# Layer 3 of a four-layer model on one core: convolutions on TensorE, two features spread by one-hot products, another order of the two lanes

## The reference, cut to what matters

```python
def _L3_attn_ref(x, ...):
    u = _rmsnorm(x, norm1_w)
    uc = conv(u, dw_kernel, 4 taps, causal, one filter per feature) + dw_bias
    xh = (uc @ pw_w.T + pw_b).reshape(b, l, 16, 8)
    xp = einsum('blhd,kd->blhk', xh, x_proj_w)          # dt_x (8), Bx (48), Cx (48)
    dt = softplus(einsum('blhr,dr->blhd', dt_x, dt_proj_w) + dt_proj_b)
    A = -exp(A_log)
    for t in range(l):
        h = exp(dt[t] * A) * h + (dt[t] * xh[t]) * Bx[t]
        y[t] = sum_s(h * Cx[t])
    x1 = x + (y @ out_proj_w.T + out_proj_b)
    h2 = _rmsnorm(x1, norm2_w)
    return x1 + (silu(h2 @ gate_w.T) * (h2 @ up_w.T)) @ down_w.T
```

## Time and profile before

| | |
|---|---|
| median of 3 runs | 2117.89 us (2117.66 to 2123.4) |
| the profiled execution | 2106.99 us |
| its span, first to last instruction | 2105.2 us |
| TensorE's mean granted clock | 0.883 of full speed |
| DMA | 113.66 MB, mean 54 GB/s |
| instructions | 28567 |

### The profile page before, as it was taken

How to read it: one execution, slowest core, us unless ns; L and a number is a source line. 1 busy time by engine, 2 the same in 40 slices (tenths; PEclk the granted TensorE clock), 3 DMA queues, 4 the chain that set the end, 5 groups by cost and what they waited for, 6 DMA issues and landing times.

```text
span 2105.2 us, 28567 instructions
## 1 busy us (share of the span) xinstructions
PE 1642.7 (78%) x10505; PEld 944.0 (45%) x10546; DVE 1371.6 (65%) x3084; ACT 909.8 (43%) x1592; POOL 799.0 (38%) x670
## 2 busy tenths in 40 slices
PE   6797698667878778876768788779768887688667
PEld 3455565112555566423335566524315455564114
DVE  4664355999554455787985435488896544467996
ACT  3462233554435333544535352344544542335553
POOL 2411101995222121373652221165571421025892
PEclk9999898777989899888889998979879998899788
DMA  6005301410000341202100312220210023302210
GB/s 197 1 1 158 99 2 35 135 41 9 13 0 1 99 129 31 85 21 64 52 1 11 99 31 61 74 93 9 85 31 6 1 59 93 98 10 85 75 52 11
DMA packets 96589, 113.66 MB, mean 54 GB/s; under 512 B 7616, under 2 KB 70848, under 8 KB 96192
## 3 DMA queue, kind: packets, MB, share of 16 engines
q1 hardware_dynamic: 94400, 107.63, 17.1%
q0 software_dynamic: 2048, 4.20, 0.7%
HBM read 88.86 MB, written 22.94 MB: 53 GB/s over the span
## 4 chain that ended last, share of the span: by engine, by line
PE 46%; DVE 19%; POOL 9%; ACT 8%; issue 7%; DMA 6%; SPq 6%; DVEq 0%; ACTq 0%; POOLq 0%
PE P L228 9%; POOL M L2079 6%; DVE M L2009 6%; PE P L1634 4%; PE P L1842 3%; SPq L1457 3%; PE P L1217 2%; SPq L1458 2%; DMA W<-in_e 2%; PE P L962 2%; PE P L2137 1%; PE P L390 1%; DMA M<-du 1%; PE P L1222 1%; PE P L217 1%
## 5 line engine op out<-in xcount | busy, mean ns | idle before, releaser
L2009 DVE TENSOR_TENSOR_SCAN M<-P,M 128x512 f32<-128x512 f32 x384 | 446.5, 1204 | 30.2 <-POOL M L2079 18.8
L1842 PE MATMUL P<-M,wt 32*32 32x512 f32 x3072 | 272.4, 780 | 144.7 <-DVE M L2009 108.4
L1923 ACT ACTIVATE P<-M,negA 128x512 f32<-128x512 f32 x384 | 264.2, 690 | 228.9 <-DVE M L2009 213.9
L228 PEld LDWEIGHTS P<-wt,M 128*128 128x128 f32 x2176 | 275.7, 193 | 97.1 <-issue 34.6
L228 PE MATMUL P<-wt,M 128*128 128x128 f32 x2176 | 289.8, 279 | 15.0 <-ACT M L1930 3.4
L2079 POOL TENSOR_TENSOR M<-M 128x512 f32<-128x512 f32 x192 | 244.0, 1305 | 138.0 <-DMA M<-du 76.1
L2079 POOL TENSOR_TENSOR M<-W,M 128x512 f32<-128x512 f32 x192 | 242.3, 1297 | 56.7 <-PE P L1842 56.5
L1842 PEld LDWEIGHTS P<-M,wt 32*32 32x32 f32 x3072 | 40.1, 117 | 330.3 <-DVE M L2009 259.0
L209 POOL TENSOR_TENSOR st<-st,wt 128x4 f32<-128x4 f32 x64 | 84.7, 1323 | 255.9 <-DVE st L192 255.5
L1731 DVE TENSOR_TENSOR M<-M,P 128x512 f32<-128x512 f32 x128 | 87.4, 683 | 93.0 <-PE P L1642 64.5
L1634 PE MATMUL P<-M,wt 128*128 128x512 f32 x256 | 138.0, 623 | 11.0 <-ACT M L1683 6.2
(11 more groups left out here) (338 smaller groups left out, 3236.0 us busy)
## 6 DMA issues: line engine op xcount, KB each, us to landing
W<-in_e SPq DMA_DIRECT2D x152, 192.0 KB
M<-dt SPq DMA_DIRECT2D x64, 256.0 KB, 5.2
M<-xs SPq DMA_DIRECT2D x32, 256.0 KB, 4.2
ys<-M SPq DMA_DIRECT2D x32, 256.0 KB, 2.3
M<-du SPq DMA_DIRECT2D x32, 256.0 KB, 4.9
W<-du SPq DMA_DIRECT2D x32, 256.0 KB, 6.0
W<-xh SPq DMA_DIRECT2D x16, 256.0 KB
xs<-zero SPq DMA_DIRECT2D x2, 1216.0 KB, 10.7
```

Source lines behind the costliest of these rows:

```text
L228: m = e.matmul(out[:, tok(j)], h[:, tok(j)], wgt, start=first and j == 0, stop=last, skip_group_check=True)
L1842: m = e.matmul(t["sums"][i // 2][to:to + 32, :], part("WC", c)[r, r], scan[r, :], start=c == 0, stop=c == 5, tile_position=(32 * i, to))
L1923: e.activation(t["aa"][n % 2][:, :], t["dtr"][i][:, :], EXP, scale=negA[:, c:c + 1]).then_inc(ACT.s, ACT.mark(b, "a3", "aa", n))
L2009: e.tensor_tensor_scan(bb[:, :], t["aa"][n % 2][:, :], bb[:, :], 0.0, MUL, ADD).then_inc(DVE.s, DVE.mark(b, "a3", "scan", n))
```

## The change

- The weights of the two convolutions are multiplied once, on DVE, into four matrices `cw` (one for each tap), and the two biases into one column `cb`. PE then computes xh with four products of `cw` and `up`, shifted by 0 to 3 columns, summed in PSUM. L1959 and L1964 go.
- ABS reads PSUM with the bias itself; z is computed behind the exponential and no longer stands ahead of it. The load of the table is issued behind xh. The last DVE steps of softplus are in another order.
- All six chunks of B are copied by ACT.
- The first two features (k = 0) of dt and du are spread by PE: products of one-hot matrices `spread` (256 columns of weights more) with `dt` and `du`, in P[0] and P[2], copied by ACT (`dtr`) and DVE (`dub`). `sp_attn3` reads back only features 2 and 3 at first.
- The bits in `TURNS` are new for all engines. "Lane 0 is favoured" means that its steps stand ahead more often.

```diff
+        cw, cb = sb("cw", [128, 512]), sb("cb", [128, 1])
@@ dve_consts
+                e.tensor_tensor(cb[:, :], L.P[3][:, 128:129], wv("pwb"), ADD).then_inc(DVE.s, DVE.mark("c", "conv"))
+                for k in range(4):
+                    e.tensor_scalar(cw[:, tok(k)], wv("pwT"), wv("dw")[:, k:k + 1], None, MUL).then_inc(
+                        DVE.s, DVE.mark("c", "conv"))
@@ pe_attn3
-            w.wait_ge(DVE.s, DVE.of(b, "a3", "conv", 3))
-            e.matmul(P[0][:, :], wv("pwT"), T_[10][:, :], start=True, stop=True).then_inc(PE.s, PE.mark(b, "a3", "xh"))
+            w.wait_ge(ACT.s, ACT.of(b, "a3", "yn"))
+            w.wait_ge(POOL.s, POOL.of(b, "a3", "pad"))
...
+            for k in range(4):
+                m = e.matmul(P[0][:, :], cw[:, tok(k)], up[:, k:k + T], start=k == 0, stop=k == 3)
+            m.then_inc(PE.s, PE.mark(b, "a3", "xh"))
...
+            for i in range(2):
+                yield
+                w.wait_ge(DVE.s, DVE.of(b, "a3", "dt"))
+                w.wait_ge(ACT.s, ACT.of(b, "a3", "dtr", 0) if i else ACT.of(b, "a3", "B", 2))
+                e.matmul(P[0][:, :], part("spread", i), T_[2][:, :], start=True, stop=True).then_inc(
+                    PE.s, PE.mark(b, "a3", "dtr", i))
+                yield
+                w.wait_ge(DVE.s, DVE.of(b, "a3", "du"))
...
+                e.matmul(P[2][:, :], part("spread", i), T_[3][:, :], start=True, stop=True).then_inc(
+                    PE.s, PE.mark(b, "a3", "dub", i))
@@ act_attn3
+            e.preload_act_table_set("natural_log_exp_and_others")
...
-            e.activation(T_[11][:, :], P[2][:, :], IDN, bias=wv("dtb")).then_inc(ACT.s, ACT.mark(b, "a3", "z"))
-            yield
-            w.wait_ge(ACT.s, ACT.of(b, "a3", "z"))
-            e.activation(T_[12][:, :], T_[11][:, :], ABS).then_inc(ACT.s, ACT.mark(b, "a3", "abs"))
+            e.activation(T_[12][:, :], P[2][:, :], ABS, bias=wv("dtb")).then_inc(ACT.s, ACT.mark(b, "a3", "abs"))
...
+            e.activation(T_[11][:, :], P[2][:, :], IDN, bias=wv("dtb")).then_inc(ACT.s, ACT.mark(b, "a3", "z"))
...
-            e.preload_act_table_set("natural_log_exp_and_others")
...
+            for i in range(2):
+                yield
+                w.wait_ge(PE.s, PE.of(b, "a3", "dtr", i))
+                e.activation(t["dtr"][i][:, :], P[0][:, :], COPY).then_inc(ACT.s, ACT.mark(b, "a3", "dtr", i))
@@ dve_attn3
+            for i in range(2):
+                yield
+                w.wait_ge(PE.s, PE.of(b, "a3", "dub", i))
+                e.tensor_copy(t["dub"][i][:, :], P[2][:, :]).then_inc(DVE.s, DVE.mark(b, "a3", "dub", i))
@@ sp_attn3
-            for q in range(4):
+            for q in range(2, 4):
                 spread(t["dtr"][q], dt_d[s], q, rep_dt[s][q])
                 spread(t["dub"][q], du_d[s], q, rep_du[s][q])
@@ TURNS, one row of "vector"
-                "9a5f5d740ff0017fffffffffff578c0be87bf480ffff9330b78000030a1fa80ee7ffdbdf3ed2405000028910f5ff3ffebffc"
+                "52dff73d55771682dfff578c0be87bf480fff87c85bf80000001e7f407e7fff5fe6ff030091204003bbf53ffebff39e0140a"
```

More of the change, by code:

```diff
@@ L1832, in gather @@
                 if g == 0:
-                    for i in (2, 3):
-                        w.wait_ge(ACT.s, ACT.of(b, "a3", "B", i))
+                    w.wait_ge(ACT.s, ACT.of(b, "a3", "dtr", 1))
+                    w.wait_ge(DVE.s, DVE.of(b, "a3", "dub", 1))
                 if k and c == 0:
@@ L1913, in decay @@
                 yield
[L1914 to L1918 removed]
+                if k == 0:
+                    w.wait_ge(ACT.s, ACT.of(b, "a3", "dtr", q))
+                elif q == i:
+                    w.wait_ge(rep_dt[b % 2][i], 16 * (b // 2 + 1))
+                else:
+                    w.wait_ge(rep_dt[b % 2][i], 16 * (2 * (b // 2) + k // 2 + 1))
+                if n == 0 and b < 2:
+                    w.wait_ge(DVE.s, DVE.of("c", "A"))
                 if n < 2:
@@ L2442, in layout @@
     add("sumd", sd)
+    add("spread", np.concatenate([(p[:, None] == p[None] // 8 * 8 + d).astype(f) for d in range(2)], 1))
     add("WB", np.concatenate([bd(xw[8 + 8 * c:16 + 8 * c].T) for c in range(6)], 1))
```

109 lines of the change are left out of this document (47 added, 62 removed).

## The result

The changed kernel takes 2067.64 us (median of 4 runs, 2064.99 to 2074.17), beside 2119.85 us for the kernel before on the same chip (4 runs, 2117.66 to 2123.4). The ratio is 0.9757, 95% interval [0.9738, 0.9776]: 52 us less. Forecast were 24 us less, 2096 us, with a range from 2062 to 2130. The sign is right, the size is under half of what came, and what the text called "a larger gain" (2070 us) is what was measured.

What follows compares the result with a forecast made beforehand. No engine is full throughout: the kernel changes between PE and DVE limits, with lanes waiting on their own chains between. Terms sum to -13.4 us, -21.4 with the order, giving 2096 us on the runs' scale; eight-in-ten range 2062 to 2130.

Steps and rivals of the forecast that it cites:

- a larger gain: Rival: the added products fall in PE's idle time, so the +26.8 us term is nothing; -48 us, 2070 us; chance 0.19.
- The ways: Layer 3 preparation, normalised input to first scan, six chain blocks: round trip -32.4, softplus -11.8, convolution +5.8 us.
- the convolution: Layer 3 preparation: four PE products replace DVE operations and one product, +1.0 us a block on the chain, +5.8 us.
- The round trip: Way from du to first scan: PE spreading replaces HBM, 9.4 to 4.0 us a block, -32.4 us; over 7 refutes.
- The softplus part: Layer 3 preparation: z and the table load leave the chain, 1.97 us in each of six blocks, -11.8 us.
- PE's share: PE's 56 added products, 58 us at 1.04 each, charged at PE's 0.46 of the chain: +26.8 us (0 to 43).
- The order: New instruction order: net 16 us less pause in one lane or the other, counted half: -8 us (-30 to +20).
- The pauses that the prediction counted: DVE order: block 3's sum no longer 40.5 us late; new pauses of 44 us at block 2's ffn3, 14.6 at block 0.
- DVE (-4.3) and ACT (+1.5): Work moved: DVE loses 22.5 us, charged at 0.19, -4.3 us; ACT gets 19 us at 0.08, +1.5 us.
- PE as the bound: Rival: 56 products cost in full beside the other lane's ffn2 and gathers; +20 to +56 us, 2148 us; chance 0.13.
- The trip was worth little: Rival: half the round trip's 32.4 us returns as another wait in the fixed order; -5 us, 2112 us; chance 0.14.
- That the new order loses: Rival: new pauses, block 2's ffn3 behind 47 scans, are not made up; +46 us, 2164 us; chance 0.04.

Runs made afterwards that it cites:

- the third run: Changed kernel with seven more products of the sixth chunk of B per block, standing on the way to the first scan: 2112.79 us, ratio 0.9985 to the kernel before.
- the fourth run: Changed kernel, its order kept, with the first two features of dt and du again through HBM: 2099.88 us, ratio 0.9893 to the kernel before.
- fifth and sixth run: Orders newly written by one list-scheduling rule: for the code of the kernel before, 2172.35 us (1.0256); for the changed code, 2128.09 us (1.004).
- the seventh run: Changed kernel with layer 3's convolution on DVE again, order kept but for 13 steps: 2109.63 us, ratio 0.9965 to the kernel before.

## Why the prediction was half right

**The ways (-32.4 - 11.8 + 5.8 = -38.4 us): two terms right, the convolution wrong.** The six blocks with a reading on the chain have ways 61.1 us shorter. The round trip gave 29.2 us of the forecast 32.4: the new way is 4.5 to 5.3 us in five of the six and 7.0 in block 7, instead of 4.0. In block 3, which was not on the chain, it is 10.3, over the bound of 7 that the prediction set, because PE's order has other work there. The softplus part gave 13.1 (forecast 11.8), though block 1 alone has 5.5 of it and block 5, which is not among the six and whose operations now stand among scans, lost 5.9. The convolution gave 18.8 and not a loss of 5.8. I added the lengths of its operations, 4.5 us with the product, but from the input to xh it lasted 5.5 to 11.5 us in seven blocks and 19.3 in block 7. Two waits of the fixed order were missing: PE's order had other products ahead of L1804 (it came 3.7 us after the last L1964 in block 2 and 3.6 us in block 3), and in block 7 the four operations stood among scans for 16.2 us.

**PE's share (+26.8 us): the step that failed.** The prediction let the seven products a block lengthen the ways (5.4 us for the four of the convolution, 1.04 to 1.68 for one in the round trip), and then charged the same 56 products once more at PE's share of the chain. They stand on the ways (all four of the spreading are in block 0's chain above), and a product there costs its length once: the third run. The share was not too high a price as such (36 us for 53.7 in f2, 37 for 40.9 in the scans, so even low), but it is for work beside the ways. Without this term the prediction's own sum is -48.2 us, 2069 us, against 2067.6. That meeting is in part luck: the same sum is off by 25 us in the convolution, and between the two kernels not all that the ways lost came out in the time. The rival "a larger gain" had this number for another reason, products in PE's idle time; the runs refute that reason.

**The order (-8 us): not a term of a sum.** Each order is worth something for its own code only: the new order costs the old code 33 us, the old order costs the new code 80. With equally refitted orders the edits are worth 37 us, and the other 15 of the 52 lie between order and code. The trace shows two things beside the ways that the prediction did not have: PE's unchanged work 38 us shorter at a higher granted clock (19 us more busy instead of 57), and DVE's L201 10 us shorter because it meets POOL less often. How much each gave was not separated by a run and stays open, and so does what kept the time from falling by as much as the ways. The pauses that the prediction counted came as read (none at block 3's sum, 45 us at block 2's ffn3), and neither can be seen in the time by itself.

**DVE (-4.3) and ACT (+1.5).** DVE's busy time fell by 25 us (forecast 22), ACT's rose by 11.5 (forecast 19); what either is worth in time was not tried alone. **The rivals.** PE as the bound is refuted by the result. "The trip was worth little" is refuted by the fourth run, 29 us. That the new order loses is refuted for the new code and true for the old, where no run shows whether its pauses are the cause.

## What to carry to other kernels

Find the way that each block must go alone and measure it end to end in the trace, not as a sum of its operations. In a fixed order a chain of short operations on an engine that serves another lane can be several times as long as alone (2.8 us became 9.7, and 16.2 in block 7 before). Moving it to another engine is one cure; standing its operations in a row took back 21 of 44 us, and in refitted orders no difference was left. Charge each moved instruction once: on the way by its length, beside the way by its share, and never both. An order written for one version of a code is no test of another; compare versions only with orders made with equal effort, and don't compare orders by their ways. Identify the block of each instruction by the program's order, not by its place in time, when two lanes share a line.

## What the runs showed of the chip

Some of VectorE's operations on SBUF lose time to GpSimd. The views of two lines in the kernel before give the spread of equal operations: L201 reaches over three times its median, the statistics of L184, on SBUF too, never do. The timelines show a slow pair of L201 beside GpSimd's multiplications:

```profile
L201 DVE TENSOR_TENSOR M<-M,st x128: 360/418/1484, 9.3 to 2086.9; 128x256 f32<-128x256 f32 x128
...
L184 DVE BATCH_NORM_STATS2 st<-xt x256: 261/276/296, 6.4 to 2084.3; 128x6 f32<-128x128 f32 x128
```

```profile
495.20 2.75 DVE L201 TENSOR_TENSOR M<-M,st 128x256 f32<-128x256 f32 x2
```

```profile
494.99 2.67 POOL L2079 TENSOR_TENSOR M<-W,M 128x512 f32<-128x512 f32 x2
```

Of 128 such operations 11 took over 1 us before, 1 in the changed kernel, 19 and 28 in the fifth and sixth run. The Trainium skill (SBUF — State Buffer, "SBUF: two separate sides") says that an operation of VectorE with two inputs in SBUF, which L201 has, and one of GpSimd that reads SBUF take a shared pair of ports as an exclusive lock, and that the later one blocks until the other is through. The trace agrees: 418 ns become up to 1484, beside GpSimd's 1.3 us. So an order decides not only when an operation runs but how long it takes.

The granted clock moves with the order of one and the same code: for the code of before 0.883 in its profiled execution, and 0.848, 0.871 and 0.876 in three other orders. In the changed kernel it is 0.902. In the seventh run the product after the 6.13 us pause took 2.08 us, where the same form takes 1.02 in block 2 of the changed kernel (L1845). The tables by stretch of the two have the granted clock behind the busy times of the five engines: half, 1.2 GHz, in a stretch in which PE was busy 0.06 of 6 us and in the one behind it, and full, 2.4 GHz, where PE was busy throughout.

```profile
415.00:421.00 6.00, 0.06 (x8) 0.00 (x0) 6.00 (x6) 2.08 (x3) 2.49 (x2) 0.50 0.00 0
421.00:424.00 3.00, 2.81 (x10) 0.73 (x18) 1.27 (x2) 0.69 (x1) 0.00 (x0) 0.50 0.00 0
```

```profile
849.00:853.00 4.00, 4.00 (x14) 1.75 (x14) 1.10 (x2) 2.92 (x6) 0.62 (x1) 1.00 0.37 135
```

So this wait of PE was paid a second time, in the length of the product behind it.
